# A new order for the last attention head, and no fetch for a head past the last one

## The reference

```python
q_hk = (hidden_q @ Wq.T).reshape(Bv, Sv, H, K)
q_big = _apply_rope(jnp.einsum('bshk,hkq->bshq', q_hk, w_kc_q), sin_q, cos_q)
q_r = jnp.einsum('bshq,hqr->bhsr', q_big, W_qr)
k_r = jnp.einsum('bld,hdr->bhlr', kv_r, W_kr)
attn = jax.nn.softmax(jnp.einsum('bhsr,bhlr->bhsl', q_r, k_r), axis=-1)
ctx_c = jnp.einsum('bhsl,bld->bhsd', attn, kv_r)
ctx_lat = jnp.einsum('bhsd,hkd->bhsk', ctx_c, w_kc_kv)
x = x + ctx_lat.transpose(0, 2, 1, 3).reshape(Bv, Sv, H * K) @ Wo.T
...
gamma_w = jnp.clip(jnp.mean(jnp.abs(w)), 1e-05, None)      # gate_w, val_w and out_w
w_dq = jnp.clip(jnp.round(w / gamma_w), -1.0, 1.0) * gamma_w
x_dq = jnp.clip(jnp.round(x * scale_x), -128.0, 127.0) / scale_x
x = x + bit_linear(silu(bit_linear(ln(x), gate)) * bit_linear(ln(x), val), out)
```

## Time and profile before

| | us |
|---|---|
| median of 3 runs | 942.2 |
| lowest and highest run | 941.69, 944.32 |
| the profiled execution, its own time | 943.72 |
| its span, first to last instruction | 941.9 |
| PE busy | 864.8 (92%) |
| DVE, ACT, POOL busy | 820.0, 535.6, 547.2 |
| mean granted clock of PE | 0.971 |

### The profile page before, as it was taken

The page is one execution under the profiler, slowest core; times in us unless marked ns, Lnnn a source line. Parts: engine busy times, 40 slices in busy tenths (PEclk is TensorE's granted clock), DMA queues, the critical chain, the costliest instruction groups (busy, mean ns, idle before and its releaser), DMA issues.

```text
span 941.9 us, 15308 instructions
## 1 busy us (share of the span) xinstructions
PE 864.8 (92%) x4280; PEld 667.6 (71%) x4290; DVE 820.0 (87%) x1208; ACT 535.6 (57%) x897; POOL 547.2 (58%) x557
## 2 busy tenths in 40 slices
PE   3557999999999999999999999999999988678996
PEld 2434788888788888788888888888888877434443
DVE  6756899989998899889998999899899977789796
ACT  2225556655665566556655665575557558884332
POOL 5186656464646464656466555646574648777562
PEclk9778999999999999999999999999999989998999
DMA  8000111102110210111011101110111036610000
GB/s 310 0 20 29 56 47 43 36 28 68 26 35 24 64 46 15 35 53 47 14 52 36 47 14 52 47 36 21 44 47 36 25 124 252 232 44 12 23 23 34
DMA packets 25176, 51.75 MB, mean 55 GB/s; under 512 B 5440, under 2 KB 11840, under 8 KB 23872
## 3 DMA queue, kind: packets, MB, share of 16 engines
q1 hardware_dynamic: 24064, 49.36, 16.3%
q10 hardware_dynamic: 1088, 2.10, 0.6%
HBM read 49.35 MB, written 2.10 MB: 55 GB/s over the span
## 4 chain that ended last, share of the span: by engine, by line
PE 78%; DVE 7%; POOL 6%; ACT 4%; issue 3%; DMA 3%; POOLq 0%; ACTq 0%; DVEq 0%; SPq 0%
PE banks L1136 43%; PE scores L1219 11%; PE banks L1202 11%; PE banks L1173 4%; PE scores L1423 4%; PE banks L1438 2%; ACT ternary L1353 1%; DMA load<-in_pack 1%; POOL raw L1348 1%; ACT probs L937 1%; POOL rot_cos L823 1%; DMA acc<-in_x 1%; ACT pt_hi L921 1%; DMA raw<-in_gate_w 1%; DVE val L1489 1%
## 5 line engine op out<-in xcount | busy, mean ns | idle before, releaser
L823 POOL TENSOR_TENSOR rot_cos<-rot_cos,rot_sin 128x512 f32<-128x512 f32 x93 | 119.9, 1290 | 146.8 <-DVE rot_sin L1034 135.2
L937 ACT ACTIVATE probs<-scores,neg_max 128x1024 f32<-128x1024 f32 x128 | 143.9, 1125 | 74.7 <-DVE neg_max L1057 74.0
L1025 DVE TENSOR_TENSOR pt_lo<-banks,pt_hi 128x512 fp32r<-128x512 f32 x256 | 164.3, 683 | 11.3 <-ACT pt_hi L921 9.1
L921 ACT CAST pt_hi<-banks 128x512 fp32r<-128x512 f32 x256 | 138.2, 596 | 54.0 <-PE banks L1202 53.8
L1057 DVE TENSOR_REDUCE neg_max<-scores 128x1 f32<-128x1024 f32 x128 | 155.8, 1218 | 10.1 <-PE scores L1219 9.2
L1202 PE MATMUL banks<-ident,probs 128*128 128x128 f32 x1024 | 134.3, 274 | 7.2 <-DVE acc L1052 3.1
L1202 PEld LDWEIGHTS banks<-ident,probs 128*128 128x128 f32 x1024 | 119.5, 141 | 26.0 <-DVE acc L1052 3.9
L831 POOL TENSOR_TENSOR rot_lo<-rot_cos,rot_hi 128x512 fp32r<-128x512 f32 x93 | 119.9, 1289 | 7.8
L1136 PE MATMUL banks<-pt_hi,v_hi 128*128 128x512 f32 x256 | 101.9, 398 | 1.3 <-DVE pt_lo L1025 1.0
L1052 DVE SCALAR_TENSOR_TENSOR acc<-banks,inv,acc 128x512 f32<-128x512 f32 x128 | 92.6, 747 | 11.7 <-PE banks L1136 9.9
L1136 PE MATMUL banks<-pt_hi,v_lo 128*128 128x512 f32 x256 | 100.0, 390 | 0.0
(11 more groups left out here) (189 smaller groups left out, 1990.2 us busy)
## 6 DMA issues: line engine op xcount, KB each, us to landing
load<-in_pack SPq DMA_DIRECT2D x15, 320.0 KB, 2.9
raw_chunk<-in_out_w SPq DMA_DIRECT2D x8, 512.0 KB, 3.9
load<-in_pack SPq DMA_DIRECT2D x16, 256.0 KB, 2.7
raw_chunk<-in_gate_w SPq DMA_DIRECT2D x8, 512.0 KB, 3.6
raw_chunk<-in_val_w SPq DMA_DIRECT2D x8, 512.0 KB, 4.2
raw<-in_gate_w SPq DMA_DIRECT2D x4, 1024.0 KB, 7.3
raw<-in_val_w SPq DMA_DIRECT2D x4, 1024.0 KB, 5.3
raw<-in_out_w SPq DMA_DIRECT2D x4, 1024.0 KB, 5.3
```

The lines of the kernel that those rows point to most:

```text
L823: nc.gpsimd.tensor_tensor(total, total, rot_sin[:, c, :], ALU.add).then_inc(rot_sum, 1)
L921: nc.scalar.copy(out, src).then_inc(group_hi, 1)
L937: nc.scalar.activation(probs[:, u % 2, :], scores[:, u % 2, :], ACT.Exp, bias=neg_max[:, u:u + 1], accum_out=sums[:, u:u + 1]).then_inc(ex ...
L1025: return nc.vector.tensor_tensor(pair[1], src, pair[0].bitcast(F32), ALU.subtract)
```

## The change

It has two parts. The three orders of the last head are written anew. And SP and GpSimd run heads 1 to 12 in their loop (six turns) and heads 13 and 14 as straight code behind it; for head 14 this code leaves out the three fetches and the two splits for head 16, and with them SP's wait for these fetches. A wait for the split of head 15's Wo stands before raw lot 2, because that slot lies over `load`. `chunk_number` and the row of a chunk get a form for heads that have no loop register. PE, ACT and DVE keep their loop of seven turns.

```diff
 LAST_PE = (
-    ("T", 7, 0, "last"), ("T", 7, 1, "last"), ("G",), ("score", 0), ("score", 1), part(0, 2, V1), ("score", 2),
-    ("score", 3), part(1, 2, V1), ("T", 0, 0), ("T", 0, 1), ("T", 1, 0), ("O", 1, 0, "last"), ("O", 1, 1, "last"),
-    ("score", 4), ("T", 1, 1), ("O", 1, 2, "last"), ("T", 2, 0), ("T", 2, 1), ("score", 5), ("T", 3, 0), ("T", 3, 1),
-    ("O", 1, 3, "last"), ("score", 6), part(0, 4, V0), ("score", 7), part(1, 4, V0), part(2, 4, V0), ("M",),
-    part(3, 4, V0), ("T", 4, 0), ("T", 4, 1), ("T", 5, 0), ("O", 0, 0), ("O", 0, 1), ("O", 0, 2), ("O", 0, 3),
-    ("T", 5, 1), ("T", 6, 0), ("T", 6, 1), ("T", 7, 0), ("T", 7, 1), part(0, 4, ("V", 1)), part(1, 4, ("V", 1)),
+    ("score", 0), ("score", 1), ("G",), ("T", 7, 0, "last"), ("score", 2), ("T", 7, 1, "last"), part(0, 2, V1),
+    part(1, 2, V1), ("T", 0, 0), ("T", 0, 1), ("T", 1, 0), ("score", 3), ("O", 1, 0, "last"), ("T", 1, 1),
+    ("O", 1, 1, "last"), ("O", 1, 2, "last"), ("score", 4), ("T", 2, 0), ("O", 1, 3, "last"), ("T", 2, 1),
+    ("score", 5), ("T", 3, 0), ("score", 6), ("T", 3, 1), ("M",), part(0, 4, V0), part(1, 4, V0), ("score", 7),
+    part(2, 4, V0), part(3, 4, V0), ("T", 4, 0), ("T", 4, 1), ("T", 5, 0), ("T", 5, 1), ("O", 0, 0), ("O", 0, 1),
+    ("O", 0, 2), ("T", 6, 0), ("T", 6, 1), ("T", 7, 0), ("O", 0, 3), ("T", 7, 1), part(0, 4, ("V", 1)),
...
 LAST_ACT = (
-    ("double", 1, "last"), ("T", 7, 0, "last"), ("T", 7, 1, "last"), ("exp", 0), ("exp", 1), ("drop", 0), V1,
-    ("T", 0, 0), ("T", 0, 1), ("T", 1, 0), ("exp", 2), ("drop", 1), ("T", 1, 1), ("exp", 3), ("T", 2, 0), ("T", 2, 1),
-    ("exp", 4), ("T", 3, 0), ("T", 3, 1), ("exp", 5), ("drop", 2), ("drop", 3), ("drop", 4), ("M",), V0, ("T", 4, 0),
-    ("T", 4, 1), ("T", 5, 0), ("exp", 6), ("drop", 5), ("T", 5, 1), ("exp", 7), ("T", 6, 0), ("T", 6, 1), ("T", 7, 0),
-    ("first root",), ("drop", 6), ("T", 7, 1), ("root", 0), ("drop", 7), ("norm", 0), ("norm", 1), ("V", 1), ("norm", 2), ("norm", 3),
-    ("first gate",), ("drop", 8), ("take", 0),
+    ("double", 1, "last"), ("exp", 0), ("T", 7, 0, "last"), ("exp", 1), ("T", 7, 1, "last"), ("drop", 0), V1,
+    ("T", 0, 0), ("T", 0, 1), ("T", 1, 0), ("drop", 1), ("T", 1, 1), ("exp", 2), ("drop", 2), ("exp", 3), ("T", 2, 0),
+    ("exp", 4), ("T", 2, 1), ("T", 3, 0), ("drop", 3), ("M",), ("exp", 5), ("T", 3, 1), ("drop", 4), ("drop", 5), V0,
+    ("T", 4, 0), ("T", 4, 1), ("T", 5, 0), ("exp", 6), ("T", 5, 1), ("drop", 6), ("exp", 7), ("T", 6, 0), ("T", 6, 1),
+    ("T", 7, 0), ("drop", 7), ("T", 7, 1), ("first root",), ("root", 0), ("norm", 0), ("norm", 1), ("norm", 2),
+    ("V", 1), ("norm", 3), ("first gate",), ("drop", 8), ("take", 0),
 )
 LAST_DVE = (
-    ("sum",), ("T", 7, 0, "last"), ("G",), ("T", 7, 1, "last"), ("max", 0), ("max", 1), ("max", 2), ("max", 3), V1,
-    ("T", 0, 0), ("T", 0, 1), ("T", 1, 0), ("O", 1, 0, "last"), ("O", 1, 1, "last"), ("max", 4), ("T", 1, 1),
...
-    ("stats", 2), ("T", 7, 1), ("stats", 3), ("spread", 0), ("deviation", 0), ("extreme", 0), ("extreme", 1), ("V", 1),
-    ("extreme", 2), ("extreme", 3), ("scale", 0), ("O", 1, 0), ("O", 1, 1), ("O", 1, 2), ("O", 1, 3),
+    ("max", 0), ("sum",), ("max", 1), ("G",), ("T", 7, 0, "last"), ("max", 2), ("T", 7, 1, "last"), V1, ("T", 0, 0),
+    ("T", 0, 1), ("max", 3), ("T", 1, 0), ("O", 1, 0, "last"), ("T", 1, 1), ("O", 1, 1, "last"), ("O", 1, 2, "last"),
+    ("max", 4), ("O", 1, 3, "last"), ("T", 2, 0), ("max", 5), ("T", 2, 1), ("T", 3, 0), ("max", 6), ("M",),
+    ("T", 3, 1), ("max", 7), V0, ("T", 4, 0), ("T", 4, 1), ("T", 5, 0), ("O", 0, 0), ("T", 5, 1), ("stats", 0),
+    ("O", 0, 1), ("O", 0, 2), ("stats", 1), ("T", 6, 0), ("T", 6, 1), ("T", 7, 0), ("O", 0, 3), ("stats", 2),
+    ("stats", 3), ("spread", 0), ("T", 7, 1), ("deviation", 0), ("extreme", 0), ("extreme", 1), ("extreme", 2),
+    ("V", 1), ("extreme", 3), ("scale", 0), ("O", 1, 0), ("O", 1, 1), ("O", 1, 2), ("O", 1, 3),
 )
...
+        def heads_of_loads(engine, prepare, period):
+
+            prepare(Period(Head(0), "prepare"))
+            period(Period(Head(0), "first"))
+            with engine.Fori(0, (H - 4) // 2) as i:
+                for odd in range(2):
+                    period(Period(Head(1 + odd, i)))
+            for n in (H - 3, H - 2):
+                period(Period(Head(n)))
...
-                for lot in (WQ, WC, WRK):
-                    load_lot(p.head.plus(2), lot)
-
-            most_heads(sp, prepare, period)
-
-            sp.wait_ge(loaded, Head(H - 1).after(64, 16 * (4 + 3) - 48))
+                if p.head.number != H - 2:
+                    for lot in (WQ, WC, WRK):
+                        load_lot(p.head.plus(2), lot)
+
+            heads_of_loads(sp, prepare, period)
             last_loads(sp)
...
             for n in range(RAW_LOTS):
+                if n == 2:
+                    sp.wait_ge(wo_ready, H)
                 raw.load(sp, n)
...
-                split_wq(p.head.plus(2))
-                split_wc(p.head.plus(2))
-
-            most_heads(pool, prepare, period)
+                if p.head.number != H - 2:
+                    split_wq(p.head.plus(2))
+                    split_wc(p.head.plus(2))
+
+            heads_of_loads(pool, prepare, period)
```

More of the change, by code:

```diff
@@ L110 @@
-    ("T", 5, 1), ("T", 6, 0), ("T", 6, 1), ("T", 7, 0), ("T", 7, 1), part(0, 4, ("V", 1)), part(1, 4, ("V", 1)),
-    part(2, 4, ("V", 1)), part(3, 4, ("V", 1)), ("O", 1, 0), ("O", 1, 1), ("O", 1, 2), ("O", 1, 3), ("X", 0),
+    ("score", 0), ("score", 1), ("G",), ("T", 7, 0, "last"), ("score", 2), ("T", 7, 1, "last"), part(0, 2, V1),
+    part(1, 2, V1), ("T", 0, 0), ("T", 0, 1), ("T", 1, 0), ("score", 3), ("O", 1, 0, "last"), ("T", 1, 1),
+    ("O", 1, 1, "last"), ("O", 1, 2, "last"), ("score", 4), ("T", 2, 0), ("O", 1, 3, "last"), ("T", 2, 1),
@@ L112 @@
+    ("score", 5), ("T", 3, 0), ("score", 6), ("T", 3, 1), ("M",), part(0, 4, V0), part(1, 4, V0), ("score", 7),
+    part(2, 4, V0), part(3, 4, V0), ("T", 4, 0), ("T", 4, 1), ("T", 5, 0), ("T", 5, 1), ("O", 0, 0), ("O", 0, 1),
+    ("O", 0, 2), ("T", 6, 0), ("T", 6, 1), ("T", 7, 0), ("O", 0, 3), ("T", 7, 1), part(0, 4, ("V", 1)),
+    part(1, 4, ("V", 1)), part(2, 4, ("V", 1)), part(3, 4, ("V", 1)), ("O", 1, 0), ("O", 1, 1), ("O", 1, 2),
+    ("O", 1, 3), ("X", 0),
 )
 LAST_ACT = (
-    ("double", 1, "last"), ("T", 7, 0, "last"), ("T", 7, 1, "last"), ("exp", 0), ("exp", 1), ("drop", 0), V1,
@@ L120 @@
 )
 LAST_DVE = (
-    ("sum",), ("T", 7, 0, "last"), ("G",), ("T", 7, 1, "last"), ("max", 0), ("max", 1), ("max", 2), ("max", 3), V1,
-    ("T", 0, 0), ("T", 0, 1), ("T", 1, 0), ("O", 1, 0, "last"), ("O", 1, 1, "last"), ("max", 4), ("T", 1, 1),
-    ("O", 1, 2, "last"), ("T", 2, 0), ("T", 2, 1), ("max", 5), ("T", 3, 0), ("T", 3, 1), ("max", 6),
-    ("O", 1, 3, "last"), ("max", 7), ("M",), V0, ("T", 4, 0), ("T", 4, 1), ("T", 5, 0), ("O", 0, 0), ("O", 0, 1),
-    ("O", 0, 2), ("O", 0, 3), ("T", 5, 1), ("stats", 0), ("stats", 1), ("T", 6, 0), ("T", 6, 1), ("T", 7, 0),
@@ L677, in chunk_number @@
         def chunk_number(h, w):
-            return (w + 1) % 3 if h.i is None else h.i * 3 + (3 + w)
+            if h.i is None:
+                return (h.number + 1) // 2 * 3 + (w if h.number else (w + 1) % 3)
+            return h.i * 3 + (3 + w)
         def most_heads(engine, prepare, period):
@@ L746, in load_chunk @@
                 if h.i is None:
-                    src = chunk_rows[w][0:P, :]
+                    k = (h.number + 1) // 2
+                    src = chunk_rows[w][k * P:(k + 1) * P, :]
                 else:
```

## The result

The changed kernel takes 939.1 us (median of 13 runs, 936.32 to 941.21), the kernel before 942.79 us in the same series (13 runs, 940.97 to 944.55). The ratio is 0.9961, 95% interval 0.9948 to 0.9973: 3.7 us faster, where 4.9 were forecast. The time lies inside the forecast's range of 935.5 to 940.9, 0.3 us under its line for "faster", 939.4.

What follows compares the result with a forecast made beforehand. Around the last head it took the chain to run through head 16's loads and splits, not PE, with ACT setting the later pace. Gains of 3.0 and 1.9 us made 942.2 - 4.9 = 937.3 us, range 935.5 to 940.9.

Steps and rivals of the forecast that it cites:

- the walk: Step-by-step timing of the last head from head 14's end to `scale`, forecast 4.9 us earlier, at 814.8.
- The fetch for head 16: On SP and GpSimd: without it, raw loads go out 7.4 us earlier and GpSimd starts 4.8 us earlier.
- the early loads don't help: Rival: GpSimd still starts at 775.0, only 0.9 to 1.3 us at the head's end remain, 941.2; chance 0.05.
- The border: Between heads 14 and 15: score tile 0 fills PE's idle time and turn 0,0 comes 3.0 us sooner.
- the clock is low at the border: Rival: PE's clock stays low there; 4.0 us gained, 938.2 (chance 0.27), or 940.5 with a longer low stretch (0.06).
- a clock that is low past 773: Sign of being wrong: PE's clock at the border between heads, expected low until about 772.5 at most in the short form.
- The half microsecond that drop 5 was to absorb: At V of batch 0, whose cast waits behind drop 5: 0.5 us absorbing some of a low clock's 1.35 us delay.
- ACT's queue: From V's cast of batch 1 on, ACT has no idle time and sets the pace; drop 0's wait costs nothing.
- a sign of being wrong: On ACT: waits for GpSimd's clips of more than 1 us after lot 0 would make the prediction wrong.
- The end of the head: On ACT: moving drop 7 from between root and first norm takes 1.89 us off the chain; `scale` comes at 814.8.
- The sum: Whole last head: 3.0 us from its first part and 1.9 from the moved drop, 4.9 us earlier in all.
- Straight code: At the loop's exit on SP and GpSimd: no cost, since GpSimd waits 10.68 us for DVE there anyway.

Runs made afterwards that it cites:

- e2: The changed kernel with the old orders of the last head, so early loads and straight code only; ratio to before 1.0007.
- e1: The kernel before with only the new orders of the last head, keeping the fetch and splits for head 16; ratio to before 0.9998.
- e5: The changed kernel with PE kept busy at the border: score tile 0 computed three times, score tile 1 twice; ratio to before 0.9955.
- e8: The changed kernel itself once more, for a second profile; ratio to before 0.9968.
- e4: The changed kernel with the gate and value bias loads issued behind raw lot 2 instead of behind lots 4 and 6; ratio to before 0.9963.
- e6: The changed kernel with drop 7 on ACT back between `root` and the first norm; ratio to before 0.9969.
- e12: The kernel before with only the new orders of the last head, a second profile; end of head 14 to `scale` took 56.1 us.
- e9: The changed kernel with drop 5 on ACT back behind exponential 6; ratio to before 0.9985.
- e3: The kernel before with heads 13 and 14 outside the loop on SP and GpSimd, keeping head 16's fetch and splits; ratio to before 0.9998.

## Why the prediction came out as it did

The time came out inside the range, and the walk behind it holds at a full clock. But the clock was low, which the forecast gave 0.33 in its two forms, and two of the reasons given for the gain were wrong.

- **The fetch for head 16.** Right: 7.4 us for the loads and 4.9 for 4.8 us for GpSimd's start, ended by DVE and not by DMA. Taken alone it is worth nothing that can be told (e2), which the forecast didn't say; its rival "the early loads don't help" priced the orders without them at 0.9 to 1.3 us, and e1's 0.9998, with an interval of 1.6 us gained to 1.3 lost, neither shows nor excludes that.
- **The border.** The order of events was as walked through. The clock was not: the rival "the clock is low at the border" is what both profiles of the changed kernel show, and the forecast's own sign of being wrong, a clock that is low past 773 (9.75 us behind the border), came true in both, with about 11.1 and 10.4 us. In stretch and turn 0,0 e5 prices it at 1.6 to 2.0 us, where the forecast had 0.9: the low stretch lasted until 776, 2 us into V. The half microsecond that drop 5 was to absorb was not there, since lot 5 is loaded only behind drop 2, and drop 2 came 1.9 us later behind the border than in the walk (its end 23.2 us for 21.3); V's cast still stood about 0.8 us behind the end of V. The Trainium skill (TensorE: Matmul & The Clock Gate, "Part 1: The HAM clock gate") says that activity releases the throttle. e5 agrees with it, 1.00 throughout with PE busy 1.79 us or more of each 2 us from 762 to 780. For one score tile in the idle time it gives no answer here: the clock fell in six executions with these PE instructions at the border (changed, e8, e4, e6, e1, e12) and stayed up in one (e9).
- **ACT's queue.** Right from V's cast of batch 1 to M: 12.9 us in the changed kernel (15.8 to 28.6 behind the border), 13.35 in the walk. GpSimd waited 4.9 and 3.9 us for lots in the two profiles, but of that ACT saw 1.0 and 1.1 us, at the limit that the forecast had named as a sign of being wrong. With e4's loads the wait at drop 5 is gone and the stretch is 0.5 to 0.8 us shorter.
- **The end of the head.** The term of 1.9 us for drop 7, which was to go from the chain, was mis-sized: in its old place the drop stands in a wait for DVE and held the norm up by 0.6 us, and ahead of turn 7,1 it costs about as much again, so the move is worth nothing (e6). That the chain of the profile shows the drop with its whole 1.89 us doesn't mean that this much goes with it. What the new order has behind V's cast is one drop less (6 and 7 for 5, 6 and 7): from V's cast to `scale` are 818.28 - 800.39 = 17.9 us, before 21.1. e9 shows this drop to be worth 2.0 us behind V's cast and 1.2 us in the whole stretch. The remaining 1.2 to 1.7 us behind V's cast (21.1 to 21.6 for 19.9) were not tested. They go with ACT's wait for DVE ahead of the root, 2.0 us in all five profiles with the old orders and in none with the new ones, where DVE finishes the statistics ahead of turn 7,1.
- **The sum.** At a full clock the stretch was forecast as 814.8 - 763.25 = 51.55 us, and e5 measured 51.5. By its own times the walk gained 1.95 us ahead of V's cast (33.35 for 35.3) and 2.9 behind it (18.2 for 21.1); its "3.0 us of it come from the first part of the head and 1.9 from the moved drop" doesn't follow from them. Measured, all of the gain lies behind V's cast (17.9 and 17.6 us), since with the low clock V's cast comes after 35.5 us, not sooner than in the old order (33.2 to 35.3 us in the four profiles with late loads). The 4.9 us were taken against the first profile's 56.4, 1 us above two later ones. The profiles give 2 to 3 us and the medians 3.0 to 3.7, with intervals that reach down to 2.5 and 1.5. The two don't contradict each other, and where a last microsecond would be stays open.
- **Straight code.** No cost that can be told, as forecast (e3: 1.4 us gained to 1.1 lost).

## What to carry to other kernels

A queue that feeds a ring of few slots and an order that consumes it have to be moved together: each alone can be worth nothing, because the lead of one becomes a wait for the other. When an instruction is moved off the chain, ask what its engine would wait for in the old place without it, and whether everything behind its new place is the same chain; only a place beside other engines' work is a gain. One profile of each kernel is not enough for a step of 1 us: repeat the profile of the kernel before too.

## What the runs showed of the hardware

The clock falls in one execution and not in the next, with the same instructions: e9 has at the border the orders of the changed kernel and kept 1.00, with PE busy 0.29 us of the 2 us from 764 and 1.20 of the next, while both profiles of the changed kernel show 0.50 there, as do e4 and e6, which share these instructions.

```profile
764.00:766.00 2.00, 0.29 (x2) 1.00 1.00 414
766.00:768.00 2.00, 1.20 (x4) 1.00 1.02 430
768.00:770.00 2.00, 1.36 (x8) 1.00 0.96 406
```

The feed-forward layer, with the same orders everywhere, took from 119.5 to 125.3 us from `scale` to the end of the span (935.0 - 815.47 in e8, 940.9 - 815.63 in e9), and 119.6 and 123.6 us both occur with the new orders and early loads (changed, e6). PE's clock in it is low at different places in each. These 4 to 6 us are more than the whole change gains. The runs of the changed kernel alone spread over 4.9 us (936.32 to 941.21), which fits; that the layer causes this spread was not tested.
